# A transformer block as 37 software-pipelined turns: the order of work on every engine laid anew

## The reference

```python
# x_q: tokens, x_kv: context, indices: 64 picks per token
q = (x_q @ W_q.T).reshape(b, nq, H, HD)               # 16 heads of 16
c_kv = x_kv @ W_kv_down.T
c_sel = c_kv[jnp.arange(b)[:, None, None], indices]
kv = (c_sel @ W_kv_up.T).reshape(b, nq, K, 2, H, HD)
scores = jnp.einsum('bqhd,bqkhd->bqkh', q, k) * SCALE
attn = jax.nn.softmax(scores, axis=2)
out = jnp.einsum('bqkh,bqkhd->bqhd', attn, v).reshape(b, nq, d)
return out @ W_out.T
# feed-forward part: gated linear attention in chunks of 64, 8 heads, DK = DV = 64
A = jnp.einsum('cthd,cshd->chts', qc * jnp.exp(g), kc * jnp.exp(-g)) * tril
o_intra = jnp.einsum('chts,cshe->cthe', A, vc)
chunk_kv = jnp.einsum('cthd,cthe->chde', kc * jnp.exp(g_last[:, None] - g), vc)
S_next = S * jnp.exp(g_last)[..., None] + kv            # scanned over the chunks
```

## Time and profile before

| what | value |
|---|---|
| median of 3 runs | 1114.73 us (1110.36, 1114.73, 1116.28) |
| span of the profiled execution, first to last instruction | 1110.1 us |
| that execution's own time | the lowest of the three, 1110.36 us, is next to its span |
| PE busy | 1057.4 us, 95% |
| DVE busy | 981.3 us, 88% |
| ACT busy | 905.9 us, 82% |
| POOL busy | 683.0 us, 62% |
| mean granted TensorE clock | 0.982 of full speed (2.4 GHz) |
| turns 0 to 5 / 6 to 32 / 33 to 36 | 148.9 / 871.4 / 89.8 us |

### The profile page before, as it was taken

One profiled execution on the slowest core, in us unless ns is written; L12 is line 12 of the kernel. 1 busy time (PEld: TensorE's weight loads), 2 busy tenths in 40 slices (PEclk: granted clock), 3 DMA queues, 4 the chain that ended last, 5 costly groups with the idle time before them and its releaser, 6 DMA issues.

```text
span 1110.1 us, 30832 instructions
## 1 busy us (share of the span) xinstructions
PE 1057.4 (95%) x11840; PEld 879.0 (79%) x11840; DVE 981.3 (88%) x2793; ACT 905.9 (82%) x2259; POOL 683.0 (62%) x707
## 2 busy tenths in 40 slices
PE   3789999999999999999999999999999999999985
PEld 2567888888888888888888888888888888888764
DVE  5779999999999999999999999999999999998643
ACT  3588888888888888888888888888888888888752
POOL 5366665566676556667665576766567676654553
PEclk8789999999999999999999999999999999999989
DMA  5432221223222222223221122222212222211111
GB/s 153 150 127 57 75 78 50 54 57 84 63 69 70 54 56 57 75 60 88 69 59 46 49 74 67 75 72 70 54 53 64 58 69 70 68 37 47 26 32 25
DMA packets 86856, 73.82 MB, mean 67 GB/s; under 512 B 34553, under 2 KB 71743, under 8 KB 86710
## 3 DMA queue, kind: packets, MB, share of 16 engines
q1 hardware_dynamic: 86134, 70.85, 24.2%
q10 hardware_dynamic: 576, 1.02, 0.3%
HBM read 37.43 MB, written 13.94 MB: 46 GB/s over the span
## 4 chain that ended last, share of the span: by engine, by line
PE 83%; DVE 7%; DMA 3%; POOL 3%; ACT 2%; SPq 1%; issue 1%; ACTq 0%; DVEq 0%; POOLq 0%
PE F L403 10%; PE TM L738 6%; PE F L874 6%; PE F L885 5%; PE F L822 5%; PE F L397 5%; PE F L849 5%; PE F L790 4%; PE F L805 3%; PE F L879 3%; PE SA L726 3%; PE F L1113 3%; PE F L763 3%; PE TM L757 3%; PE F L866 3%; PE F L833 3%
## 5 line engine op out<-in xcount | busy, mean ns | idle before, releaser
L733 DVE CUSTOM_DVE_ANT_0 SA<-SA,LNC 128x154 f32<-128x154 f32 x512 | 146.1, 344 | 11.5 <-PE SA L726 9.8
L2168 POOL COPY X1B<-X 128x256 f32<-128x256 f32 x27 | 13.9, 516 | 149.3 <-DVE X L1434 149.3
L738 PEld LDWEIGHTS TM<-CONST,EXPS 128*128 128x128 f32 x512 | 74.5, 208 | 27.3 <-issue 24.8
L719 DVE TENSOR_REDUCE PACKED<-HOT 128x19 int32<-128x1216 bf16 x64 | 92.3, 1443 | 0.0
L738 PE MATMUL TM<-CONST,EXPS 128*128 128x128 f32 x512 | 89.8, 299 | 2.3 <-ACT EXPS L1769 1.3
L733 DVE DVE_READ_ACCUMULATOR2_ANT MAXS<- 128x1 f32 x512 | 70.0, 137 | 0.0
L874 PE MATMUL F<-QM,STATE 128*64 128x128 f32 x1024 | 64.7, 280 | 2.9 <-POOL QM L2229 1.8
L874 PEld LDWEIGHTS F<-QM,STATE 128*64 128x64 f32 x1024 | 56.8, 139 | 13.3 <-POOL QM L2195 8.3
L2163 POOL TENSOR_TENSOR LS<-LS,ZABS 128x1024 f32<-128x1024 f32 x27 | 63.9, 2366 | 4.7 <-ACT ZABS L1914 3.8
L885 PE MATMUL F<-WO,OG 128*128 128x256 f32 x256 | 63.6, 391 | 2.2 <-DVE OG L1524 2.0
L403 PEld LDWEIGHTS F<-XMT,WQ 128*128 128x128 f32 x512 | 63.9, 196 | 1.8
(11 more groups left out here) (536 smaller groups left out, 3840.8 us busy)
## 6 DMA issues: line engine op xcount, KB each, us to landing
QD<-QG SPq DMA_DIRECT2D x128, 128.0 KB, 2.3
QS<-q_dram SPq DMA_DIRECT2D x64, 192.0 KB, 3.1
q_dram<-QPARTS SPq DMA_DIRECT2D x32, 192.0 KB, 2.2
XA<-x_dram SPq DMA_DIRECT2D x32, 128.0 KB, 2.2
QS<-q_dram SPq DMA_DIRECT2D x32, 128.0 KB, 3.1
XB<-x_dram SPq DMA_DIRECT2D x32, 128.0 KB, 3.0
out_dram<-OUT SPq DMA_DIRECT2D x32, 128.0 KB, 1.7
EG<-EGP SPq DMA_DIRECT2D x128, 4.0 KB, 1.8
```

Of the source, the lines that this page charges most:

```text
L719: return dve.tensor_reduce(PACKED[:, r], HOT[:, r, :], AX.X, ALU.add)
L733: last = dve.tensor_tensor_reduce(s, s, LNC[t % 2][:, :], -1.0, LARGE, ALU.add, ALU.min, out[:, h:h + 1])
L738: pe.transpose(TA[:, cols(hh)], exps[:, 0:P, hh], ident)
```

## The change

Every operation of a tile stays the same, with the same operands. What changes is the order in which each engine's queue has them, in all three versions, and with it the semaphores: most shared counters (`s_a_index`, `s_c_hidden`, `s_b_scores`) are split, and each wait names the count that the new order needs. In the steady turns:

- PE: the gate products go ahead of the second scores; the transposes of EXPS 1 go from behind V to behind the third scores; `inner(KG2T)` goes ahead of the fourth scores; `z_features` goes from behind the transposes of EXPS 0 to directly behind `kv_products`; `scores(a, 0)` goes ahead of `dense_kv_products`. The RMS product waits for one half of STATE, `dense_kv_products` for the other.
- POOL: ZREST goes from ahead of `decays` to behind `decays`, STATE and QPARTS2; ZPARTS2 goes behind STATED; the cast of IDX goes from ahead of QREST to the turn's end, and X1B with it.
- SP: XB and XA are loaded between the `eg_move` DMAs; HIDG between the QD ones; the q store and the load of IDX go ahead of the z stores; of the z slabs, 0 goes ahead of the q slabs, and 2 and 1 go behind them and HIDK.
- ACT: ZPARTS0 goes behind LOGIT; ZPARTS1 stands between the second and third EXPS of scores 2, the fourth EXPS behind that and a PT copy, and the fourth scores wait for it (`s_b_exps`).

In turns 0 to 5, the work for the first V rows stands ahead of the first K rows on PE and ahead of the first q product, the K loads stand behind the landing of the q store, and a group of weights is loaded at the end of turn 2. In turns 33 to 36, `kv_products` stands behind `z_features`.

The core of the diff, of the steady turns:

```diff
 def pe_tiles(l, a, b, c, d, e):
-    pe.wait_ge(s_a_xt, c + 3)
     pe.wait_ge(s_c_xm, c + 1)
     transposes(C0, XM[:, :], KD).then_inc(s_c_xmt_ps, 1)
-    scores(b, 1).then_inc(s_b_scores, 1)
-    pe.wait_ge(s_c_sigm, d + 1)
     gate_products(LS3[d % 2], CUME[d % 2]).then_inc(s_d_g2_ps, 1)
+    pe.wait_ge(s_b_exps0_0, b + 1)
+    scores(b, 1).then_inc(s_b_b, 1)
     pe.wait_ge(s_c_xmt, a - 1)
...
     pe.wait_ge(s_d_at2, d + 1)
     kv_products(VM[d % 2])
+    pe.wait_ge(s_c_zslabs, 48 * c + 48)
+    pe.wait_ge(s_c_v, c + 1)
+    z_features().then_inc(s_c_z0_ps, 1)
     pe.wait_ge(s_b_ot, 2 * b + 1)
     exp_transposes(EXPS[:, 0]).then_inc(s_b_exps_ps, 1)
-    pe.wait_ge(s_c_v, c + 1)
-    pe.wait_ge(s_c_zslabs, 48 * c + 48)
-    z_features().then_inc(s_c_z0_ps, 1)
     pe.wait_ge(s_d_at, d + 1)
-    inner_outputs(V[d % 2]).then_inc(s_d_o_inner, 1)
-    pe.wait_ge(s_b_probs, 2 * b + 2)
-    pe.wait_ge(s_b_exps1_3, b + 1)
...
+    pe.wait_ge(s_d_states_0, 2 * d + 1)
...
-def pool_tiles(l, a, b, c, d, e):
...
-    pool.tensor_tensor(QREST[:, :, :], QT[:, :, :], QPARTS[:, 0, :, :], ALU.subtract).then_inc(s_a_qrest, 1)
-    pool.wait_ge(s_c_zparts, 2 * c + 1)
-    pool.tensor_tensor(ZREST[:, :], HID2[:, :], ZPARTS[:, 0, :], ALU.subtract).then_inc(s_c_zrest, 1)
-    if l < TILES:
-        pool.wait_ge(s_a_index, 5 * l + 2)
-        pool.tensor_tensor(IW[1][:, :], IW[1][:, :], IW[0][:, :], ALU.add).then_inc(s_a_index, 1)
-    pool.wait_ge(s_d_egd, 64 * d + 64)
-    decays(d).then_inc(s_d_dec, 1)
-    pool.wait_ge(s_c_zparts, 2 * c + 2)
-    pool.tensor_tensor(ZPARTS[:, 2, :], ZREST[:, :], ZPARTS[:, 1, :], ALU.subtract).then_inc(s_c_zrest, 1)
-    pool.wait_ge(s_d_dec, d + 1)
-    pool.tensor_tensor(states, states, DEC[:, 0:NS].unsqueeze(2).to_broadcast([P, NS, DK]), ALU.mult)
-    pool.tensor_tensor(STATED[:, :, :], STATED[:, :, :], DEC[:, NS:NS + NP].unsqueeze(2).to_broadcast([P, NP, DK]), ALU.mult)
-    pool.tensor_tensor(QPARTS[:, 2, :, :], QREST[:, :, :], QPARTS[:, 1, :, :], ALU.subtract).then_inc(s_a_qrest, 1)
-    pool.wait_ge(s_d_qd, 64 * d + 64)
-    pool.tensor_tensor(QM[:, 0, :, :, :].rearrange("p a b t -> p (a b) t"), QD[:, :, :, :].rearrange("p a b t -> p (a b) t"), ISEXPT[d % 2][:, 0, :].unsqueeze(1).to_broadcast([P, H, P]), ALU.mult)
...
+def pool_tiles(l, a, b, c, d, e):
...
+    pool.wait_ge(s_a_qparts, 2 * a + 1)
+    pool.tensor_tensor(QREST[:, :, :], QT[:, :, :], QPARTS[:, 0, :, :], ALU.subtract).then_inc(s_a_qrest, 1)
+    pool.wait_ge(s_d_egd, 64 * d + 64)
+    decays(d).then_inc(s_d_dec, 1)
+    pool.wait_ge(s_d_dec, d + 1)
+    pool.tensor_tensor(states, states, DEC[:, 0:NS].unsqueeze(2).to_broadcast([P, NS, DK]), ALU.mult)
+    pool.wait_ge(s_a_qparts, 2 * a + 2)
+    pool.tensor_tensor(QPARTS[:, 2, :, :], QREST[:, :, :], QPARTS[:, 1, :, :], ALU.subtract).then_inc(s_a_qrest, 1)
+    pool.wait_ge(s_c_zparts, 2 * c + 1)
+    pool.tensor_tensor(ZREST[:, :], HID2[:, :], ZPARTS[:, 0, :], ALU.subtract).then_inc(s_c_zrest, 1)
+    pool.tensor_tensor(STATED[:, :, :], STATED[:, :, :], DEC[:, NS:NS + NP].unsqueeze(2).to_broadcast([P, NP, DK]), ALU.mult)
+    pool.wait_ge(s_c_zparts, 2 * c + 2)
+    pool.tensor_tensor(ZPARTS[:, 2, :], ZREST[:, :], ZPARTS[:, 1, :], ALU.subtract).then_inc(s_c_zrest, 1)
+    pool.wait_ge(s_d_qd, 64 * d + 64)
+    pool.tensor_tensor(QM[:, 0, :, :, :].rearrange("p a b t -> p (a b) t"), QD[:, :, :, :].rearrange("p a b t -> p (a b) t"), ISEXPT[d % 2][:, 0, :].unsqueeze(1).to_broadcast([P, H, P]), ALU.mult).then_inc(s_d_qm_2, 1)
...
 def sp_tiles(l, a, b, c, d, e):
+    sp.wait_ge(s_d_exp2, d + 1)
+    eg_move(d, 1, 1).then_inc(s_d_egd, 16)
+    eg_move(d, 0, 1).then_inc(s_d_egd, 16)
+    sp.dma_start(XB[:, :], x[rows(b), :]).then_inc(s_b_load_xb, 16)
+    eg_move(d, 1, 0).then_inc(s_d_egd, 16)
+    if l < TILES:
+        sp.dma_start(XA[:, :], x[rows(l), :]).then_inc(s_l_load_xa, 16)
+    eg_move(d, 0, 0).then_inc(s_d_egd, 16)
+    sp.wait_ge(s_d_q2, d + 1)
+    sp.dma_start(QD[DK * 0:DK * 0 + DK, 1, :, :], QG2[DK * 1:DK * 1 + DK, :, :]).then_inc(s_d_qd, 16)
+    sp.wait_ge(s_c_hidden_logit, 2 * c + 1)
+    sp.dma_start(HIDG[DK:P, :], HID2[0:DK, :]).then_inc(s_c_hidg, 16)
+    sp.dma_start(QD[DK * 1:DK * 1 + DK, 0, :, :], QG2[DK * 0:DK * 0 + DK, :, :]).then_inc(s_d_qd, 16)
+    sp.dma_start(QD[DK * 1:DK * 1 + DK, 1, :, :], QG2[DK * 1:DK * 1 + DK, :, :]).then_inc(s_d_qd, 16)
+    sp.dma_start(QD[DK * 0:DK * 0 + DK, 0, :, :], QG2[DK * 0:DK * 0 + DK, :, :]).then_inc(s_d_qd, 16)
+    sp.wait_ge(s_a_qrest, 2 * a + 2)
+    sp.dma_start(q_dram.rearrange("(n p) w -> p n w", n=PARTS), QPARTS[:, :, :, :].rearrange("p n k t -> p n (k t)")).then_inc(s_a_qstore, 16)
     if l < TILES:
         sp.dma_start(IDX[:, :], idx[rows(l), :]).then_inc(s_l_load_idx, 16)
-        sp.wait_ge(s_a_xn, l)
-        sp.dma_start(XA[:, :], x[rows(l), :]).then_inc(s_l_load_xa, 16)
-    sp.wait_ge(s_d_exp2, 2 * d + 1)
-    eg_move(d, 1, 0).then_inc(s_d_egd, 16)
-    eg_move(d, 0, 0).then_inc(s_d_egd, 16)
-    eg_move(d, 0, 1).then_inc(s_d_egd, 16)
-    eg_move(d, 1, 1).then_inc(s_d_egd, 16)
-    sp.wait_ge(s_d_q2, d + 1)
-    sp.dma_start(QD[DK * 0:DK * 0 + DK, 1, :, :], QG2[DK * 1:DK * 1 + DK, :, :]).then_inc(s_d_qd, 16)
-    sp.dma_start(QD[DK * 1:DK * 1 + DK, 1, :, :], QG2[DK * 1:DK * 1 + DK, :, :]).then_inc(s_d_qd, 16)
-    sp.dma_start(QD[DK * 0:DK * 0 + DK, 0, :, :], QG2[DK * 0:DK * 0 + DK, :, :]).then_inc(s_d_qd, 16)
-    sp.dma_start(QD[DK * 1:DK * 1 + DK, 0, :, :], QG2[DK * 0:DK * 0 + DK, :, :]).then_inc(s_d_qd, 16)
-    sp.wait_ge(s_c_hidden, 3 * c + 2)
+    sp.wait_ge(s_c_zrest, 2 * c + 2)
+    z_store(0).then_inc(s_c_zstore, 16)
+    z_store(1).then_inc(s_c_zstore, 16)
+    sp.wait_ge(s_c_zstore, 32 * c + 32)
+    z_slabs(0).then_inc(s_c_zslabs, 16)
+    sp.wait_ge(s_a_qstore, 16 * a + 16)
+    q_slabs(2, QS[a % 2]).then_inc(s_a_qslabs, 16)
+    q_slabs(1, QS[a % 2]).then_inc(s_a_qslabs, 16)
+    q_slabs(0, QS[a % 2]).then_inc(s_a_qslabs, 16)
     sp.dma_start(HIDK[0:DK, :], HID1[DK:P, :]).then_inc(s_c_hidk, 16)
-    sp.wait_ge(s_c_zrest, 2 * c + 2)
-    z_store(1).then_inc(s_c_zstore, 16)
-    z_store(0).then_inc(s_c_zstore, 16)
-    if a >= 4 and (a + 4) % TPB < 5 and a + 4 < B * TPB:
+    z_slabs(2).then_inc(s_c_zslabs, 16)
+    z_slabs(1).then_inc(s_c_zslabs, 16)
+    if a >= 4 and (a + 4) % TPB < 5 and (a + 4 < B * TPB):
         sp_batch((a + 4) // TPB, (a + 4) % TPB)
-    sp.wait_ge(s_a_qrest, 2 * a + 2)
-    sp.dma_start(q_dram.rearrange("(n p) w -> p n w", n=PARTS), QPARTS[:, :, :, :].rearrange("p n k t -> p n (k t)")).then_inc(s_a_qstore, 16)
-    sp.wait_ge(s_c_zstore, 32 * c + 32)
-    z_slabs(2).then_inc(s_c_zslabs, 16)
-    z_slabs(0).then_inc(s_c_zslabs, 16)
-    z_slabs(1).then_inc(s_c_zslabs, 16)
-    sp.wait_ge(s_a_qstore, 16 * a + 16)
-    q_slabs(1, QS[a % 2]).then_inc(s_a_qslabs, 16)
-    sp.dma_start(XB[:, :], x[rows(b), :]).then_inc(s_b_load_xb, 16)
-    q_slabs(2, QS[a % 2]).then_inc(s_a_qslabs, 16)
-    q_slabs(0, QS[a % 2]).then_inc(s_a_qslabs, 16)
-    sp.dma_start(HIDG[DK:P, :], HID2[0:DK, :]).then_inc(s_c_hidg, 16)
+    sp.wait_ge(s_c_by_label, c + 1)
+    sp.dma_start(HQ[c % 2][DK:P, :], HQ[c % 2][0:DK, :]).then_inc(s_c_hqd, 16)
     sp.wait_ge(s_e_out, d + 1)
     sp.dma_start(out[rows(d), :], OUT[:, :]).then_inc(s_e_store, 16)
-    sp.dma_start(HQ[c % 2][DK:P, :], HQ[c % 2][0:DK, :]).then_inc(s_c_hqd, 16)
```

1679 lines of the change are left out of this document (819 added, 860 removed).

## The result

The changed kernel takes 1348.8 us (median of 4 runs, 1346.7 to 1352.6) against 1112.8 for the kernel before in the same comparison: a ratio of 1.213 (1.210 to 1.216), slower by 236 us. The prediction said slower, 1265 us, in a range that ended at 1310. The sign and the place were right, the size was not. The profiled execution has a span of 1345.6 us, 235.5 above the 1110.1 of before.

A forecast was written before the change was run, and what follows sets the result against it. PE alone was taken to bound the steady turn. From the 1110.1 us span: +105 z chain, +54 clock falls, −5 gains, +3 first six turns, −2 last four = +155, 1265 us; range 1198 to 1310.

The forecast's parts named there:

- the signs listed at the end of the prediction: Profile after: PE busy near 85%, 2.5 to 3.5 us idle before `z_features`, ZREST near 9.1, turns 36 us or more, PEclk below 1.00.
- Step 1: SP's EG DMAs, with XB and XA between at 0.46 us each: last EG issued at 4.5, landed 1.8 later, at 6.3.
- Step 2: POOL and ACT: DEC, STATE 1.9, QPARTS2, ZREST, then ZPARTS1 hidden behind STATED; ZPARTS2 done at 10.5, called 3.8 us later.
- Step 3: SP: z stores at 10.5 and 11.0, landed 13.4; last z slab issued at 16.0, landing at 18.2 by the 2.2 us.
- Step 4: Landing of z slabs behind the larger q slabs: 18.3 taken, bounds 17.8 and 19.3; 3.9 us a turn, 105 us.
- The clock: PE falls to half clock behind the gaps in 16 of 27 steady turns, 3.4 us each: 54 us (0 to 92).
- The rival without the clock: Same z chain stall, 2.8 us PE gap without falls to half clock: 1211 us (1198 to 1238), chance 0.28.
- The gains: Steady turns on PE: RMS product needing one half of STATE, and earlier gate, 0.1 us each a turn: minus 5 us (0 to 8).
- First six and last four: First six turns +3 us (−5 to +6), first scores later; last four −2 (−4 to +1), STATE's halves saving 0.6 in two turns.
- the chain is in time: Rival: last z slab lands before PE stands at 14.4, so PE stays the bound: 1106 us (1099 to 1111), chance 0.06.
- it is late by a little: Rival: EG or stores land sooner, stall 0.2 to 1.2 us a turn, clock holds: 1115 to 1143 us, chance 0.07.
- effects cancel: Rival: gains of 0.2 a turn against a first six worse by 6: within 0.5% of before, chance 0.04.

The follow-up runs named there:

- y1: Kernel before with only z slabs 2 and 1 issued behind the q slabs on SP, steady turns: 1225.8 us, ratio 1.103.
- x1: Changed kernel with z slabs 2 and 1 put back ahead of the q slabs, steady turns: 1259.4 us, 1.133 to the kernel before.
- x3: Changed kernel with nine unused 512-column products added on PE ahead of the wait for the z slabs: 1385.0 us, 1.245 to the kernel before.
- x5: Changed kernel with five unused 512-column products added on PE ahead of the wait for the z slabs: 1320.5 us, 1.187 to the kernel before.
- y4: Kernel before with ZREST and ZPARTS2 behind STATE and QPARTS2 on POOL, and z slabs 2 and 1 behind the q slabs: 1247.1 us, ratio 1.121.
- x8: Changed kernel with the old z chain order, XA loaded first on SP and the HOT product directly behind K on DVE: 1155.1 us, 1.039 to before.
- z1: Kernel before with STATE's halves signalled one by one and scores(a, 0) ahead of dense_kv_products: 1113.2 us, ratio 1.0005.
- x2: Changed kernel with STATED put behind ZPARTS2 on POOL, steady turns: 1333.3 us, 1.199 to the kernel before.
- x6: Changed kernel with the old z chain order in the steady turns and XA's load first in SP's list: 1168.9 us, 1.052 to the kernel before.

## Why the prediction was right or wrong

**The bound.** Right: PE alone set the steady turn, so an order could only lose, and with the change it lost on the one chain that was added up. `z_features` waits for ZS in all 27 turns, ZREST stands behind QPARTS2, PE is busy in 83% of the span, and the signs listed at the end of the prediction are there, with larger numbers.

**The z chain, step by step.** This is the step that failed, a term of the sum that was mis-sized: 18.3 was forecast for the start of `z_features`, 21.4 was measured. Offsets of after are means over the 27 steady turns.

| step | predicted | measured | missed, in total |
|---|---|---|---|
| last EG issued | 4.5 | 5.01 | 0.5 |
| DEC starts (EG landed) | 6.3 | 7.27 | 1.0 |
| ZREST starts (STATE, QPARTS2 before it) | 9.1 | 10.47 | 1.4 |
| ZPARTS2 done, first z store | 10.5 | 13.04 | 2.5 |
| stores landed, slab 0 issued | 13.4 | 15.74 | 2.3 |
| last slab issued | 16.0 | 18.47 | 2.5 |
| landed, `z_features` | 18.3 | 21.4 | 3.1 |

Step 1: XB and XA were taken at 0.46 each, half of the pair of z stores. They take 0.64 from issue to issue, the pace of the EG DMAs around them, and so did the row that stood nearest, had it been used (2.57 for four); XA takes more in 7 turns. DEC starts 2.3 behind the last EG, not 1.8; no run tells why. Step 2 took durations from rows in which the operation ran beside nothing that holds it. STATED was taken as hiding ACT's ZPARTS1 in 0.6 us, and took 1.89 in most turns (1.75 in the mean); STATE took 2.23 instead of 1.90, begun while DVE's product for K ran (650.81 to 651.53 in the turn shown). Together they make 1.6 of the 3.1. (The "3.8 us later" of this step counts from the start of ZPARTS2 to its end; from end to end it is 3.4. The sum doesn't use it.) Step 3 was right: 2.4 us from the second store to slab 0, 2.7 from there to the last slab. Step 4: the landing was put at 2.3, "near the 2.2, since the z slabs are small", with the 3.3 of the q slabs as the bound. It was 2.9. y1 shows the same place without the rest of the change: 3.25 behind the q slabs, against 2.2 in turn 34 of before with nothing large near, and 2.5 in x1 where the q slabs follow.

The Trainium skill's page DMA: Bandwidth & Descriptors ("Queues, rings and completion order") had named the rule against this step: the semaphore write of a DMA lands behind all earlier writes of the same DMA engine. The measured 2.9 (after) and 3.25 (y1) behind the q slabs, against 2.5 (x1) ahead of them, go its way; that they come from this rule and not from the large DMAs taking the same engines' time is not shown. By 0.6 us a turn, 17 us in all, the prediction was too low here. The 2.5 of x1, where nothing large is ahead, is not explained by the rule.

By the measured chain this term is (21.4 − 14.4) × 27 = 189 us, forecast 105.

**The clock.** Right in size: 54 forecast, 50 measured by the rest of the turn (19.14 against the 17.28 of x3 and x5). It was forecast as 16 falls at 3.4 us each; it is 29 stretches, 164 us long in all, about one in each turn, and each costs 1.7 us (50 over 29). The longer gap brought more falls, and a fall cost less because the stretches are shorter (5.6 us in the mean, against 6.9) and in part idle. Two errors so cancel here: that the sum of this term came out near is luck. The Trainium skill's page TensorE: Matmul & The Clock Gate ("HAM oscillation — how this bites in real kernels") would have had a fall in every turn, and that is what the trace of after shows; in y1, with waits of 3.0 us at `z_features` in the mean (82.0 in 27), it is 20 in 27 turns, in y4, with 2.0 (47.9 in 24), 17. The rival without the clock is out: x5 shows the clock's own price.

**The gains.** At full clock the rest is 17.28, against 17.15 + 0.70 = 17.85 for the same work before: 0.57 a turn, 15 us in all, where 5 had been put. But no gain is shown by it, for the first part has grown by about as much. In x8, at full clock, PE is busy for 14.80 us of a turn ahead of `z_features` and for 17.38 from it on; in before, with the transposes of EXPS 0 counted to the second part, for 14.41 and 17.78. The sum is 32.18 and 32.19 us. The order moved time from one side of `z_features` to the other and saved none, so the 15 us below are an item of the account only. That is also why z1, whose expectation was built on the shorter rest, found nothing in the steady turns.

**First six and last four.** +7.7 and +4.3, forecast +3 and −2. The first scores start at 27.08 instead of 23.48, 3.6 later, for which 3 had been forecast. After, on PE, POOL, DVE and SP in turn:

```profile
27.08 0.67 PE L721 MATMUL SA<-KNOW,QS 128*128 128x154 bf16 x4 [11.59 <-DMA QS<-q_dram]
```

```profile
14.56 1.84 POOL L2067 TENSOR_TENSOR QREST<-QT,QPARTS 128x256 f32<-128x256 f32 x1 [2.03 <-ACT QPARTS L1669]
```

```profile
14.43 1.45 DVE L1324 TENSOR_TENSOR HOT<-HOT,WEIGHT 128x2496 bf16<-128x2496 bf16 x1
```

```profile
17.63 0.37 SPq L2231 DMA_DIRECT2D q_dram<-QPARTS  x1
```

HOT stands ahead there and holds QREST for 1.2 us, and the q store with it. The prediction had HOT down for its own length in DVE's queue only. The further loss is that turns 3 to 5 have the steady z wait already (ZS 3.4 and 2.3 us), and so have turns 33 and 34 (7.4 us in two waits, 0.7 before): the stage terms were summed as if the new z chain began and ended with the steady turns. By z1 the halves of STATE save 3.2 us in the last four turns, where 2 had been put; the z wait there outweighs it.

**The sum.** 189 + 50 − 15 + 7.7 + 4.3 = 236, against 105 + 54 − 5 + 3 − 2 = 155. Of the 81 us missed, 84 are the z chain's. **The range** failed by the same step: its upper end took the landing of the slabs and the falls at their bounds, and every duration on POOL as if it couldn't vary. With STATED's hold (1.1 us in the mean) and the landing (0.6) at what they measured, 47 us more, the forecast would have been 1312.

**The rivals.** That the chain is in time, that it is late by a little, and that effects cancel are out by after's own trace. What was missing among them is one that makes the forecast worse: the same chain, held on POOL by DVE.

## What to carry to other kernels

Where one engine is busy all the time, a new order can only lose: add up each chain that crosses engines, issue by issue through every queue it passes, and give a DMA that something waits for its place ahead of large ones on which nothing waits yet. Take the durations on POOL and DVE with what the other engine runs at that moment, as moving an operation moves it into other company. A wait of some microseconds on PE can be paid twice, once as idle time and again at half clock: here 4.6 us a turn, and 1.9 on top.

## What the runs showed of the hardware

POOL and DVE hold each other. In after STATED took 1.89 instead of 0.61 us, in x2 ZPARTS2 1.25 instead of 0.42, in x6 QPARTS2 1.89 instead of 0.67, in x8 ZREST 1.57 instead of 0.43, in turn 1 of after QREST 1.84 instead of 0.67, each started while DVE's 1.44 us product of HOT ran, and each ended 0.3 to 0.5 us behind it. Out of that product's way they are back at their own length: STATED at 0.61 in x2, QPARTS2 at 0.67 in x8. In the kernel before, it was to be seen already, where it cost nothing. DVE and POOL of before:

```profile
567.47 1.44 DVE L1448 TENSOR_TENSOR HOT<-BASE,BASETAB 128x2496 bf16<-128x2496 bf16 x1
```

```profile
567.85 1.16 POOL L2173 CAST IW<-IDX 128x64 f32<-128x64 int32 x1 [0.75 <-DMA IDX<-idx_dram]
```

The cast takes 0.24 us in after, where it stands alone (the turn at 643.20 has it at 663.80). The Trainium skill's page SBUF — State Buffer ("SBUF: two separate sides") states that a VectorE instruction with two SBUF inputs and a GpSimd instruction that reads SBUF lock each other out, and whichever starts first has it to its end. All these places agree with it, and so does HOT's 1.88 us in x6, started inside STATE.

A small DMA lands later next to large ones. From the issue of the last z slab to the start of the waiting `z_features` it was 2.2 us where nothing large was near (turn 34 of before, one case), 2.5 and 2.6 in the mean where the q slabs followed (x1, x6), 2.9 behind the q slabs and HIDK (after), and 3.25 and 3.3 directly behind the q slabs (y1, y4).

The clock also fell where PE's gaps were smaller than those of the earlier trace rows. In y4 a wait of 1.9 us for EXPS in the mean and one of 2.0 for the slabs went with 17 stretches at half clock in the steady turns; in x1 waits of 2.1 us (53.0 in 25, none above 3.2), with 0.9 and 0.7 us ahead of them, with 21; in x6 waits of 1.5 us alone (none above 2.7) with one. The prediction had called its own gaps "between these rows but nearer to the first two"; in x1 and y4 the mean gaps were smaller than those, and the clock fell in most turns all the same. Whether that hangs on the other gap ahead of them in the same turn was not tried.
